# Rows written out one by one instead of looped in a transformer kernel for one core

## The reference

```
x = x + attention0(norm(x))        # 16 heads of 8, causal
x = x + experts0(norm(x))          # 8 experts of 256, gated by the best two
x = x + linear_attention(norm(x))  # 16 heads, elu + 1
x = x + transformer1(norm(x))      # 6 layers, see below
x = x + rotary_attention(norm(x))  # 1 head of 128, causal
x = x + transformer2(norm(x))      # 6 layers, other weights
x = x + latent_attention(norm(x))  # 16 heads, low-rank q, k, v, causal
x = x + block3(norm(x))            # full attention, then 8 experts of 512, best one
```

```
for i in range(6):
    x = attn_layer(shift_tokens(x), Wqkv[i], q_scale[i], k_scale[i], Wo[i]) + x
    x = ffn_layer(shift_tokens(x), ln_g[i], ln_b[i], W1[i], b1[i], W2[i], b2[i]) + x
```

## Time and profile before

| | before |
|---|---|
| median of 3 runs | 6849.57 us (6849.34 to 6857.63) |
| the profiled execution | 6845.91 us |
| its span | 6844.1 us |
| mean granted clock of TensorE | 0.937 |
| TensorE busy | 5781.3 us, 84% of the span |
| VectorE busy | 4301.4 us, 63% |
| ScalarE busy | 4181.1 us, 61% |
| GpSimd busy | 2489.0 us, 36% |
| code for TensorE (queue q8) | 187 packets, 3.06 MB |
| code for the others (queue q14) | 394 packets, 3.23 MB |
| data (queue q1) | 45.65 MB, 2.0% of the DMA engines' time |

### The profile page before, as it was taken

The page is one execution under the profiler, slowest core; times in us unless marked ns, Lnnn a source line. Parts: engine busy times, 40 slices in busy tenths (PEclk is TensorE's granted clock), DMA queues, the critical chain, the costliest instruction groups (busy, mean ns, idle before and its releaser), DMA issues. The chain is left out here.

```text
span 6844.1 us, 138815 instructions
## 1 busy us (share of the span) xinstructions
PE 5781.3 (84%) x41538; PEld 4245.0 (62%) x41538; DVE 4301.4 (63%) x17058; ACT 4181.1 (61%) x14046; POOL 2489.0 (36%) x2090
## 2 busy tenths in 40 slices
PE   8885798988989889897498898988989899787989
PEld 7773465665656656565266565666656667566878
DVE  4453775767767677675476775767767576444432
ACT  5511675767757577574286675857758586445643
POOL 0000553545545454451254553545445353000000
PEclk9995999999999999998699999999999999889999
DMA  0000000000000000000000000000000000000000
GB/s 9 19 0 2 19 1 18 2 14 5 1 18 1 14 5 14 4 1 3 18 1 14 5 0 18 1 14 5 12 6 1 17 1 1 4 0 3 0 25 6
DMA packets 22293, 51.95 MB, mean 8 GB/s; under 512 B 6728, under 2 KB 16208, under 8 KB 19536
## 3 DMA queue, kind: packets, MB, share of 16 engines
q1 hardware_dynamic: 21712, 45.65, 2.0%
HBM read 44.60 MB, written 1.05 MB: 7 GB/s over the span
## 5 line engine op out<-in xcount | busy, mean ns | idle before, releaser
L1518 PE MATMUL bank<-wA,next_rowT 128*128 128x512 f32 x2304 | 1271.0, 664 | 296.7 <-DVE turnB L1770 204.9
L1615 POOL TENSOR_TENSOR turnA<-raw,ropes 128x512 f32<-128x512 f32 x768 | 970.7, 1273 | 1042.2 <-ACT raw L1665 1000.6
L1638 ACT ACTIVATE pairs<-pairs,negmax 128x128 f32<-128x128 f32 (+1 forms) x3072 | 1249.0, 431 | 53.5 <-DVE negmax L1731 51.4
L1731 DVE CUSTOM_DVE_ANT_0 pairs<-bank,bands,rs 128x128 f32<-128x128 f32 (+1 forms) x3072 | 945.8, 364 | 266.8 <-PE bank L1450 255.1
L1622 POOL TENSOR_TENSOR qk<-turnA,turnB 128x512 f32<-128x512 f32 x768 | 969.7, 1273 | 0.0
L1518 PEld LDWEIGHTS bank<-wA,next_rowT 128*128 128x128 f32 x2304 | 390.7, 197 | 800.8 <-DVE turnB L1770 470.3
L1647 ACT ACTIVATE pairsT<-bank 128x256 f32<-128x256 f32 x1536 | 521.4, 404 | 477.9 <-PE bank L1463 436.2
L252 POOL TENSOR_TENSOR rstd<-vareps,neg_half 128x2 f32<-128x2 f32 x152 | 106.5, 701 | 1798.2 <-DVE vareps L241 1798.2
L1638 ACT ACTIVATION_READ_ACCUMULATOR pairs<-pairs,negmax 128x1 f32 x3072 | 663.7, 216 | 0.0
L1628 POOL TENSOR_TENSOR qk<-qk,rs 128x1024 f32<-128x1024 f32 x192 | 365.4, 1903 | 733.2 <-DVE recip L1788 733.2
L1770 DVE TENSOR_TENSOR turnB<-bank,ropes 128x512 f32<-128x512 f32 x768 | 522.8, 681 | 0.0
(11 more groups left out here) (266 smaller groups left out, 11877.7 us busy)
## 6 DMA issues: line engine op xcount, KB each, us to landing
wA<-in_wt_wqkv SPq DMA_DIRECT2D x12, 1536.0 KB, 6.2
wB<-in_wt_wo SPq DMA_DIRECT2D x12, 512.0 KB, 3.3
wC<-in_wt_w SPq DMA_DIRECT2D x12, 341.0 KB, 3.0
wD<-in_wt_w SPq DMA_DIRECT2D x12, 192.0 KB, 2.9
big<-in_e_up SPq DMA_DIRECT2D x1, 2048.0 KB
big<-in_e_down SPq DMA_DIRECT2D x1, 2048.0 KB
scl<-in_wt_scales SPq DMA_DIRECT2D x12, 128.0 KB, 6.3
X<-in_x SPq DMA_DIRECT2D x8, 128.0 KB, 2.5
```

Source lines behind the costliest of these rows:

```text
L1518: pe.matmul(chunk_bank(i)[:, :], c.next_rowT[:, t * P:(t + 1) * P], wqkv[:, k * 512:(k + 1) * 512], start=True, stop=True).then_inc(s.chun ...
L1615: g.tensor_tensor(c.turnA[:, m % 2, :].rearrange("p (h d) -> p h d", h=8), c.raw[:, m % 4, :].rearrange("p (h d) -> p h d", h=8), cos, ALU ...
L1638: last = a.activation(tile, tile, ACT.Exp, scale=-1.0, bias=c.negmax[:, 2 * p + side, t:t + 1], accum_out=c.pair_sums[:, p % 4, t, side:si ...
L1731: last = v.tensor_tensor_reduce(c.pairs[:, 2 * (p % 4) + side, AT[t]:AT[t] + SPAN[t]], c.bank[side][:, AT[t]:AT[t] + SPAN[t]], c.bands[:, ...
```

## The change

Every loop over rows is replaced by a Python `for`, which writes the rows' instructions into the program one after another, on TensorE, ScalarE, VectorE and GpSimd. This touches the seven stages that are not transformers (loops of 7 or 8 turns), and the pair loops inside both transformers. The loops over layers stay, on all engines, and so does the whole program of SyncE. What an engine computes and in which order is as before; branch, compare and counter go, and where no layer loop stands around a row, the waits' numbers turn from registers into constants. The written program gets longer: TensorE from 6006 to 13546 instructions, VectorE from 4614 to 9105, ScalarE from 2541 to 5164, GpSimd from 1051 to 1665. The body of a layer loop now has 2112 instructions on TensorE, 1671 on VectorE, 941 on ScalarE and 451 on GpSimd.

```diff
--- before.py
+++ after.py
@@ -628,13 +628,13 @@
                                      stop=True)
                 last.then_inc(out_in_psum, 1)
 
-            with pe.Fori(0, B - 1) as b:
+            for b in range(B - 1):
                 one_row(b, False)
             one_row(B - 1, True)
 
         @block.gpsimd
         def _(g):
-            with g.Fori(0, B) as b:
+            for b in range(B):
                 norm.pool(g, b)
 
         @block.scalar
...
@@ -676,7 +676,7 @@
                 if not final:
                     step.end()
 
-            with v.Fori(0, B - 1) as b:
+            for b in range(B - 1):
                 one_row(b, False)
             one_row(B - 1, True)
 
...
@@ -1962,9 +1962,8 @@
                     pe_scores(pe, turn, 0, 0, True)
                     pe_scores(pe, turn, 0, 1)
                     pe_window(pe, turn, 0, first=True)
-                    with pe.Fori(0, B // 2 - 1) as pair:
-                        pe_window(pe, turn + pair * 2 + 1, 1)
-                        pe_window(pe, turn + pair * 2 + 2, 0)
+                    for b in range(1, B - 1):
+                        pe_window(pe, turn + b, b % 2)
                     pe_window(pe, turn + B - 1, 1, last=True)
                     pe.wait_ge(s.ff_weights, d * n_ff + n_ff)
                     for b in range(B):
@@ -1994,10 +1993,9 @@
                 def layer(d, last):
                     for slot in range(PAIRS):
                         pool_prepare(g, d * B + 1, 1, 1, slot)
-                    with g.Fori(1, B // 2) as pair:
-                        for j in range(2):
-                            for slot in range(PAIRS):
-                                pool_prepare(g, d * B + pair * 2 + j, pair * 2 + j, j, slot)
+                    for b in range(2, B):
+                        for slot in range(PAIRS):
+                            pool_prepare(g, d * B + b, b, b % 2, slot)
                     pool_ff(g, d * B, 0)
                     for b in range(B):
                         if b + 1 < B:
@@ -2023,9 +2021,8 @@
                     act_probs(a, turn, 0, 0)
                     act_probs(a, turn, 0, 1)
                     act_window(a, turn, 0, first=True)
-                    with a.Fori(0, B // 2 - 1) as pair:
-                        act_window(a, turn + pair * 2 + 1, 1)
-                        act_window(a, turn + pair * 2 + 2, 0)
+                    for b in range(1, B - 1):
+                        act_window(a, turn + b, b % 2)
                     a.wait_ge(s.ff_weights, d * n_ff + n_ff)
                     act_window(a, turn + B - 1, 1, last=True)
                     a.activation(c.cols[:, 30:31], c.neg_half[:, 0:1], ACT.Gelu)
@@ -2070,9 +2067,8 @@
                     dve_negmax(v, turn, 0, 0)
                     dve_negmax(v, turn, 0, 1)
                     dve_window(v, turn, 0, 0, first=True)
-                    with v.Fori(0, B // 2 - 1) as pair:
-                        dve_window(v, turn + pair * 2 + 1, pair * 2 + 1, 1)
-                        dve_window(v, turn + pair * 2 + 2, pair * 2 + 2, 0)
+                    for b in range(1, B - 1):
+                        dve_window(v, turn + b, b, b % 2)
                     dve_window(v, turn + B - 1, B - 1, 1, last=True)
                     v.wait_ge(s.ff_weights, d * n_ff + n_ff)
                     step = None if last else dve_steps(v, turn + B)
```

More of the change, by code:

```diff
@@ L854, in one_row @@
                         last.then_inc(hidden_ready, 1)
-            with a.Fori(0, B - 1) as b:
+            for b in range(B - 1):
                 one_row(b, False)
@@ L975, in _ @@
             pe.wait_ge(loaded, 64)
-            with pe.Fori(0, B) as b:
+            for b in range(B):
                 norm.tensor(pe, b)
@@ L1010, in _ @@
             a.activation(c.cols[:, 30:31], c.neg_half[:, 0:1], ACT.Exp)
-            with a.Fori(0, B) as b:
+            for b in range(B):
                 norm.scalar(a, b)
@@ L1021, in _ @@
             v.wait_ge(loaded, 64)
-            with v.Fori(0, B) as b:
+            for b in range(B):
                 step = Steps(v, step_v, b, LN_STEPS + 3)
```

2 lines of the change are left out of this document (1 added, 1 removed).

## The result

The changed kernel took 6796.52 us (median of 4 runs, 6792.98 to 6800.37) against 6849.45 us of the kernel before (4 runs): 53 us less, ratio 0.9923 with a 95% interval of 0.9905 to 0.9940. Its profiled execution took 6798.74 us, 47.2 less than the one shown of before.

What follows compares the result with a forecast made beforehand. The prediction took the ring of waits inside a row as the bound, TensorE being busy 84%. Its terms, 57.9 + 1.6 + 4 = 63.5 us, brought 6849.6 to 6786 us, range 6764 to 6813.

Steps and rivals of the forecast that it cites:

- the likeliest case: Whole kernel: the forecast itself, 6786 us, own range 6766 to 6806; chance 80%.
- the marks: Local attention: six L1794 instructions per layer, spanning five rows; forecast 41.0 us apart, 205.0 us in all, after the change.
- Term 1: Pair loops in both transformers' local attention: writing them out removes the back edges' excess over 41.0 us rows, 57.9 us.
- The ruler: VectorE's L1794, one instruction per row of local attention; its distances, 41.0 us without a back edge, price the edges.
- Its account of the causes: Pair loops' edges: VectorE's 2.4 us instruction-fetch stall; up to 5 us an edge where ScalarE stalls beside it, otherwise 0.9.
- Streaming costs 0.0 us a row: Local attention: written-out code is fetched without delay, since rows with and without q8 packets both take 41.0 us.
- Rival A: Local attention: fetching written-out code stops TensorE, 2.20 us a packet, 211 us added, total 6997 us; chance 4%.
- Term 2: Last layer of each transformer: waits against constants instead of registers save 0.13 us for each of 12 rows, 1.6 us.
- Term 3: Eight-row stages outside the transformers: only the first experts stage gains, 0.6 us a row over 7 rows, 4 us taken.
- The layers' own back edge stays, with TensorE's 2.20 us: Edges between layers: loops stay, TensorE's 2.20 us stall unchanged; GpSimd's longer body may miss, covered by twelve microseconds.
- The blur: Unchanged parts of the layers: shifting half-clock stretches move ten parts by 2 us each, 20 us either way.
- Rival B: Local attention: half of each edge's excess turns up at block borders elsewhere, gain only 32 us, 6818 us; chance 8%.

Runs made afterwards that it cites:

- layers_too: The changed kernel with the loops over layers also written out on TensorE, GpSimd, ScalarE and VectorE: 6736.4 us, ratio 0.9824.
- pairs_only: The kernel before with only the pair loops inside the two transformers written out, on all four engines, the seven other stages keeping their loops: 6803.9 us, ratio 0.9928.
- layers_pe_kept: The changed kernel with the loops over layers written out on VectorE, ScalarE and GpSimd, TensorE keeping its own: 6762.2 us, ratio 0.9873.

## Why the prediction came out as it did

6786 was forecast, 6796.5 measured, inside 6764 to 6813: the likeliest case and its sign were right, 10 us too far. By the profiled executions 63.5 us were forecast and 47.2 came: the marks fell short by 1.9 us, the parts between them grew by 15.7 and the end by 1.4, and the stages in front gave 2.6 more than forecast. That the medians miss by 10 us and the profiled executions by 16 is chance. By its steps:

**Term 1, 57.9 us: measured 57.6, or 58.8 without the 1.2 us that belong to term 2.** The ruler was the right instrument. It prices an edge whatever causes the loss, so the sum held although my account of the causes was incomplete.

**Its account of the causes: partly wrong.** "The first pays up to 5 because ScalarE stalls beside it" names one of three. In layers 0 to 4 there were VectorE's second stall too (ten times, 9.8 us, in the list that I had read only for L1740) and stretches of half clock, 1.7 to 5.1 us of a layer by the same estimate. And I read all of it as the price of looping. The runs show that most of it was the price of where the loops lay: moved code alone removed 37 of the 47 us of the first transformer. What is the loop's own is VectorE's 2.4 us before L1740, which came at every place tried and costs 1.1 to 2.1 us a layer.

**"Streaming costs 0.0 us a row": right.** TensorE now fetches its code in every row, 358 packets in place of 187, and the marks didn't mind. Rival A is out.

**Term 2, constants, 1.6 us: wrong in sign.** Layers 5 and 11 take 205.5 us where the layers with registers take 204.9, and layers_too has 205.5 everywhere; a row is 41.11 against 40.98 us. The 0.1 us read off was the row behind the loop, and I carried it over to rows of another kind. It is 1.2 us more, not 1.6 less. That the constants themselves are the cause isn't shown: rows with registers took 41.22 us in pairs_only, more than those with constants. In layers_pe_kept TensorE's layer loop alone was enough to bring the marks from 205.5 back to 205.0.

**Term 3, 4 us: measured 7.1.** By the row it was right (0.6 forecast, 0.70 measured at equal clock, in five rows of seven); the rest is two rows at full clock, which nothing in the term foresaw. That the gap before L880 falls from 0.52 us to next to nothing was as forecast:

```profile
428.82 0.42 DVE L930 TENSOR_TENSOR X<-X,ctx 128x256 f32<-128x256 f32 x1
429.28 0.17 DVE L880 COPY small<-bank 128x16 f32<-128x16 f32 x1
```

The second experts stage gave nothing: seven rows take 216.3 us before and after.

**"The layers' own back edge stays, with TensorE's 2.20 us": incomplete.** It stayed in the first transformer (3.7 us from the last addition to the first L1731), but in the second VectorE's own return became the later one: 4.18 us of idle, the edge 1.0 us longer at each of four edges, 4 us in all. Of these, 1.4 are TensorE's product starting later and 2.6 are VectorE coming after it; with VectorE's layer loop written out and TensorE's kept (layers_pe_kept) the edges are at 3.2 to 3.9 us again. I had looked there for GpSimd's longer body, which shows 1.0 us of idle at most, and not for VectorE's. I had also counted ten such edges; there are eight.

**The blur, 20 us either way: it came out at 11 us, the wrong way.** Of the 15.7 us by which the parts between the marks grew, 4 are those edges (4.6 with the first transformer's). The other 11 go with half clock, for which the estimate gives 244 us instead of 227, more than enough. That there was more of it is shown, in one profiled execution of each kernel; why these stretches fell so isn't. The term had the right size, and nothing known then gave it a sign.

**Rival B, "the stall only moves", true in a small part.** The excess of the rows went whole. Its argument, that code can be late in straight code too, just behind an edge, holds: VectorE's second stall of the kernel before was one, and in the changed kernel VectorE has a second stall of 1.6 to 1.7 us behind each layers' edge of the second transformer. But what came on at these edges is 4 us, not 32.

## What to carry to other kernels

When an engine idles with "issue" behind a loop's back edge, price it by the distance between marks of the whole ring (the engines waiting for one another in turn), with and without the edge, and read every "issue" entry of every engine, the short second ones too. An entry whose idle time was there before under another name is not a stall. Then test the place before the loop: a few useless instructions ahead of it can remove a stall or bring one, so a gain from writing out one stage may come from moving another, and a kernel's loops should be looked at again after every edit in front of them. Where the waits of an engine are long enough to hide its loops, leave them; here VectorE and ScalarE in local attention were worth writing out, and the loops over layers: TensorE's is worth 21 us at the edges, those of the other three went with 39 us less, most of it in the granted clock.

## What the runs showed of the hardware

- Equal loops stalled at each edge in one place and at none in another: ScalarE's pair loop in the first transformer, 22 stalls of 1.5 to 2.3 us, and none after its code was moved by 64 instructions (24 and 14 packets of q14 in the six marks of layer 2). VectorE's stall of 2.3 to 2.7 us before L1740 came at all 24 edges in each of the eight kernels that kept its pair loop, 396 instructions a turn.
- Total code fetched says little. The queue of the other engines moved 394 packets before and 395 after, and 287 with everything written out. The packets between two marks say more.
- Waits against constants do not come out cheaper than against registers in every ring: with the loop gone too, a row of the experts stage gained 0.70 us, but a row of local attention took 41.11 us with constants and 40.98 to 41.22 with registers.
- The same instructions took 197.1 to 208.0 us in the unchanged part of a layer: 2.7 to 3.7 us of that is the layers' edge (3.6 to 4.7 us in the changed kernel, 0.97 without one), most of the rest goes with the granted clock. I could not foresee how it falls from the profile of before, and over a run it weighed 11 us, more than the 6.6 that the stages in front gained.
